# Sparse first FFN on eight group buffers, with late weights and zeros sent later and its block stages one tick further apart

## The reference, cut to what matters

```python
x = L0_attn_x
x = x + 0.5 * ffn(layernorm(x))
x = x + attn(layernorm(x))
x = x + 0.5 * ffn(layernorm(x))

def ffn(x):   # 8 experts, 2 of them per token
    w = softmax(x @ router_w + router_b)                    # [.., 8]
    gate = top-2 of w, divided by their sum, 0 elsewhere
    h = gelu(einsum('btd,nde->btne', x, W1) + b1)           # 256 -> 128 per expert
    out = einsum('btne,nef->btnf', h, W2) + b2              # 128 -> 256
    return sum(out * gate[..., None], axis=-2)
```

## Time and profile before

| what | before |
|---|---|
| median of 3 runs | 2168.53 us |
| the profiled execution | 2167.86 us |
| its span, first to last instruction | 2166.1 us |
| sparse first layer (ends with the last output product) | 0 to 424 us |
| first scatters, then batch 0's end of scatters | 30 us, 84 us |
| batch 1's, batch 2's end of scatters | 190 us, 313 us |
| mean granted PE clock over the span | 0.957 |

### The profile page before, as it was taken

One profiled execution on the slowest core, in us unless ns is written; L12 is line 12 of the kernel. 1 busy time (PEld: TensorE's weight loads), 2 busy tenths in 40 slices (PEclk: granted clock), 3 DMA queues, 4 the chain that ended last, 5 costly groups with the idle time before them and its releaser, 6 DMA issues.

```text
span 2166.1 us, 39513 instructions
## 1 busy us (share of the span) xinstructions
PE 1909.9 (88%) x12240; PEld 1479.5 (68%) x12240; DVE 1526.4 (70%) x5026; ACT 1220.3 (56%) x3005; POOL 1195.1 (55%) x1376
## 2 busy tenths in 40 slices
PE   3576777888998988988988988988999999999998
PEld 3576766856666656656656656655767688888887
DVE  4566577676685685685686686686674478888887
ACT  3354566847546547547547547547556545555554
POOL 5785666467276276277277277277245444444444
PEclk9987888989998999999999999999999999999999
DMA  9755567411030031031031031031013101111110
GB/s 329 279 195 187 208 218 225 170 52 38 6 101 27 1 103 30 1 103 30 1 103 31 1 103 30 1 103 30 1 45 127 34 23 40 40 40 40 40 40 30
DMA packets 106696, 173.74 MB, mean 80 GB/s; under 512 B 13409, under 2 KB 65017, under 8 KB 105593
## 3 DMA queue, kind: packets, MB, share of 16 engines
q1 hardware_dynamic: 83304, 117.37, 16.0%
q0 software_dynamic: 20736, 52.52, 7.9%
q10 hardware_dynamic: 2448, 1.33, 0.2%
HBM read 80.33 MB, written 90.84 MB: 79 GB/s over the span
## 4 chain that ended last, share of the span: by engine, by line
PE 43%; POOL 20%; DVE 16%; issue 14%; ACT 3%; DMA 2%; SPq 1%; DVEq 0%; POOLq 0%; ACTq 0%
PE bank L705 7%; PE bank L707 6%; PE bank L706 6%; PE bank L977 4%; PE bank L959 4%; PE bank L948 4%; POOL prob L1933 3%; PE bank L988 3%; POOL spots_d L1882 3%; POOL hs_d L1920 3%; PE bank L919 3%; DVE x L1516 2%; POOL y_row L1904 2%; POOL z_row L1904 2%; DVE st L1353 1%
## 5 line engine op out<-in xcount | busy, mean ns | idle before, releaser
L1933 POOL TENSOR_TENSOR prob<-prob,rden 128x512 f32<-128x512 f32 x320 | 337.5, 1057 | 483.3 <-DVE rden L1722 480.2
L1264 ACT ACTIVATE prob<-prob,nmax 128x256 f32<-128x256 f32 x512 | 256.3, 504 | 365.4 <-DVE nmax L1704 365.2
L1704 DVE CUSTOM_DVE_ANT_0 prob<-bank,mask 128x256 f32<-128x256 f32 x512 | 195.1, 418 | 154.5 <-PE bank L948 154.2
L1591 DVE SCALAR_TENSOR_TENSOR xb<-bank,gate,xb 128x256 f32<-128x256 f32 x512 | 211.9, 476 | 55.6 <-PE bank L707 54.9
L959 PE MATMUL bank<-ident,prob 128*128 128x128 f32 x1280 | 201.9, 282 | 49.0 <-POOL prob L1933 49.0
L959 PEld LDWEIGHTS bank<-ident,prob 128*128 128x128 f32 x1280 | 157.3, 144 | 110.2 <-POOL prob L1933 69.6
L948 PE MATMUL bank<-kT,qT 64*128 64x256 f32 x1024 | 211.6, 434 | 23.2 <-DVE nmax L1704 18.4
L1858 POOL TENSOR_TENSOR hl<-hf,hh 128x512 fp32r<-128x512 f32 x128 | 164.6, 1291 | 113.5 <-ACT hh L1088 108.8
L1716 DVE COPY probT<-bank 128x512 f32<-128x512 f32 x160 | 110.2, 689 | 119.9 <-PE bank L959 119.8
L1087 ACT ACTIVATE hf<-bank,b1s 128x512 f32<-128x512 f32 x128 | 88.2, 689 | 171.2 <-PE bank L707 167.7
L977 PE MATMUL bank<-probT,V 128*64 128x128 f32 x2048 | 172.6, 290 | 0.5 <-ACT oT_s L1280 0.5
(11 more groups left out here) (254 smaller groups left out, 5511.7 us busy)
## 6 DMA issues: line engine op xcount, KB each, us to landing
xin<-spots_d SPq DMA_DIRECT2D x85, 256.0 KB, 3.9
made_d<-yout SPq DMA_DIRECT2D x85, 256.0 KB, 3.2
xb<-in_L_attn_x SPq DMA_DIRECT2D x16, 512.0 KB, 4.4
x<-in_L_attn_x SPq DMA_DIRECT2D x8, 1024.0 KB, 6.3
x_d<-x SPq DMA_DIRECT2D x8, 1024.0 KB, 5.0
xb<-x_d SPq DMA_DIRECT2D x16, 512.0 KB, 3.8
out<-xb SPq DMA_DIRECT2D x16, 512.0 KB, 2.9
spots_d<-zeros SPq DMA_DIRECT2D x24, 256.0 KB, 3.0
```

The lines of the kernel that those rows point to most:

```text
L1264: act.activation(prob[j % NP][:, h, :], src, ACT.Exp, bias=nmax[:, j % 4, h:h + 1], scale=-1.0 if light else 1.0, accum_out=den[:, j % 4, ...
L1591: dve.scalar_tensor_tensor(out=x, in0=bank[ob][:, (t % 2) * D:(t % 2 + 1) * D], scalar=gate[:, k % 2, t, e:e + 1], in1=x, op0=ALU.mult, op ...
L1704: ins = dve.tensor_tensor_reduce(prob[j % NP][:, h, :], bank[g % NS][:, 0:KEYS], mask[:, which, :], -1.0, 3e38, ALU.add, ALU.min, nmax[:, ...
L1933: pool.tensor_tensor(prob[j % NP][:, :, :], prob[j % NP][:, :, :], rden[:, j % 4, :].unsqueeze(2).broadcast_to([P, 2, KEYS]), ALU.mult).th ...
```

## The change

- The groups get eight buffers `xb` in place of four. A group from the ninth on is loaded six ticks ahead of its own tick, once the scatters of the group eight before have landed; groups 6 and 7 share space with staged weights and wait for their split.
- The groups' ticks move: 3 apart up to group 6, then 4, 6 and 5 apart. The last group's tick is 61 in place of 63, `STEP0` 24 in place of 25.
- A group's stages are further apart: `rstd` 1, norm 2, transposes 3, logits 4, route 5, exponential 6, spots on PE 6, spots and gates on DVE 7, scatters 8 to 11.
- A step's stages: transposes and `xh` 0, the copy of W1 and `xl` 1, hidden 2, gelu 3, `hl` 4, output 5, `yout` 6, store 7; `xh` and `xl` get a third buffer. There are 117 ticks in place of 115. On PE the order in a tick is transposes, output, hidden, group jobs.
- SP: the staged attention weights go to tick 7, the broadcast of b2 from ACT's queue to SP's tick 11, the three transfers of zeros to ticks 13, 36 and 60, the late attention weights to ticks 82 and 86, the store of the split weights from tick 12 to 90, the load of row 0 from 24 to 70.
- Three of row 0's projections are made in ticks 112 to 114, in place of two. The copy of token numbers into `yr` comes after the ticks.

The diff, cut to its core (buffer indices `% 4` become `% 8` for `xb`, and `% 2` become `% 3` for `xh` and `xl`, in all other places too):

```diff
-        xb = [at(f"xb{i}", [P, TG, D], F32, xt_off + i * TG * D * 4) for i in range(4)]
+        xb_off = [xt_off + i * TG * D * 4 for i in range(4)] + [y_off, y_off + TG * D * 4] + [yr_off + (T * (D + 1) + i * TG * D) * 4 for i in range(2)]
+        xb = [at(f"xb{i}", [P, TG, D], F32, off) for i, off in enumerate(xb_off)]
...
-        xh = [at(f"xh{i}", [P, C, BLK], F32R, x1_off + (T * D + i * C * BLK) * 4) for i in range(2)]
-        xl = [at(f"xl{i}", [P, C, BLK], F32R, x1_off + (T * D + (2 + i) * C * BLK) * 4) for i in range(2)]
+        x_off = [x1_off + T * D * 4, x1_off + (T * D + 2 * C * BLK) * 4, yr_off]
+        xh = [at(f"xh{i}", [P, C, BLK], F32R, x_off[i]) for i in range(3)]
+        xl = [at(f"xl{i}", [P, C, BLK], F32R, x_off[i] + C * BLK * 4) for i in range(3)]
...
-        STEP0 = 25
-        TICKS = STEP0 + STEPS + 5
-        GROUP_AT = (0, 4, 8, 12, 16, 20, 24, 27, 30, 34, 38, 43, 48, 53, 58, 63)
+        STEP0 = 24
+        TICKS = STEP0 + STEPS + 8
+        GROUP_AT = (0, 3, 6, 9, 12, 15, 18, 22, 26, 30, 36, 41, 46, 51, 56, 61)
         def group_at(tau, after):
...
         DOT0 = at_ticks(11, 12, 13, 14, 15, 16, 17, 18)
-        QKV0 = {STEP0 + STEPS + 1 + i: i for i in range(2)}
+        QKV0 = {STEP0 + STEPS + 3 + i: i for i in range(3)}
         def tick_jobs(tau):
-            jobs = [("aT", k, pr) for k in group_at(tau, 2) for pr in range(2)]
+            jobs = [("aT", k, pr) for k in group_at(tau, 3) for pr in range(2)]
             jobs += [("alg", k, 0) for k in group_at(tau, 4)]
             jobs += [("apos", k, 0) for k in group_at(tau, 6)]
             jobs += [("zt", 0, i) for i in ZT0.get(tau, ())]
...
         def attn_jobs(u):
-            jobs = [("qkv", b, i) for b, i in due(u, qkv_slot, 25) if (b, i) not in ((0, 0), (0, 1))]
+            jobs = [("qkv", b, i) for b, i in due(u, qkv_slot, 25) if (b, i) not in ((0, 0), (0, 1), (0, 2))]
             jobs += [("srow", b, i) for b, i in due(u, srow_slot, 4)]
...
         def sent(engine, n):
-            for k in range(2 * BATCH[n][1] - 4, 2 * BATCH[n][1]):
-                engine.wait_ge(s_sc[k % 4], 128 * (k // 4 + 1))
+            for k in range(2 * BATCH[n][0], 2 * BATCH[n][1]):
+                engine.wait_ge(s_sc[k % 8], 128 * (k // 8 + 1))
...
-                if k >= 4:
-                    sp.wait_ge(s_sc[k % 4], 128 * (k // 4))
-                sp.dma_start(xb[k % 4][:, :, :], half(x_v, k)).then_inc(s_xa[k % 4], 16)
+                if k in (6, 7):
+
+                    sp.wait_ge(s_wlo, 4)
+                if k >= 8:
+                    sp.wait_ge(s_sc[k % 8], 128 * (k // 8))
+                sp.dma_start(xb[k % 8][:, :, :], half(x_v, k)).then_inc(s_xa[k % 8], 16)
             def pads(n):
...
             group_load(3)
-            sp.dma_start(wqkv_st[:, :, :], wqkv.rearrange("(c p) n -> p c n", p=P)).then_inc(s_wld[4], 16)
-            sp.wait_ge(s_const, CONST)
-            for n in range(len(BATCH)):
-                sp.dma_start(spots_d[n][SPARE[n]:SPARE[n] + (E - 1) * BLK, :].rearrange("(j p s) d -> p j (s d)", p=P, s=BT),
-                             zeros[:, :, :].rearrange("p s d -> p (s d)").unsqueeze(1).broadcast_to([P, E - 1, BT * D])).then_inc(s_spare, 16)
-            sp.dma_start(wqh_s[:, :, :], wq_h.rearrange("(c p) n -> p c n", p=P)).then_inc(s_late, 16)
-            sp.dma_start(wkvh_s[:, :, :], wkv_h.rearrange("(c p) n -> p c n", p=P)).then_inc(s_late, 16)
-            sp.dma_start(wol_s[:, :, :], wo_l.rearrange("(c p) n -> p c n", p=P)).then_inc(s_late, 16)
-            sp.dma_start(woh_s[:, :, :], wo_h.rearrange("(c p) n -> p c n", p=P)).then_inc(s_late, 16)
             for tau in range(TICKS):
-                for s_ in step_at(tau - 5):
+                for s_ in step_at(tau - 7):
                     block_store(s_)
                 for s_ in step_at(tau + 3):
                     block_load(s_)
-                for k in group_at(tau, 10):
-                    if k + 4 < GROUPS:
-                        group_load(k + 4)
-                if tau == 12:
+                for k in group_at(tau + 6, 0):
+                    if k >= 4:
+                        group_load(k)
+                if tau == 7:
+                    sp.dma_start(wqkv_st[:, :, :], wqkv.rearrange("(c p) n -> p c n", p=P)).then_inc(s_wld[4], 16)
+                if tau == 11:
+                    sp.dma_start(b2_all[:, :, :].rearrange("p e n -> p (e n)"), b2.rearrange("(a e) n -> a (e n)", a=1).broadcast_to([P, E * D])).then_inc(s_b2all, 16)
+                if tau in (13, 36, 60):
+
+                    if tau == 13:
+                        sp.wait_ge(s_const, CONST)
+                    n = (13, 36, 60).index(tau)
+                    sp.dma_start(spots_d[n][SPARE[n]:SPARE[n] + (E - 1) * BLK, :].rearrange("(j p s) d -> p j (s d)", p=P, s=BT),
+                                 zeros[:, :, :].rearrange("p s d -> p (s d)").unsqueeze(1).broadcast_to([P, E - 1, BT * D])).then_inc(s_spare, 16)
+                if tau == 82:
+                    sp.dma_start(wqh_s[:, :, :], wq_h.rearrange("(c p) n -> p c n", p=P)).then_inc(s_late, 16)
+                    sp.dma_start(wkvh_s[:, :, :], wkv_h.rearrange("(c p) n -> p c n", p=P)).then_inc(s_late, 16)
+                if tau == 86:
+                    sp.dma_start(wol_s[:, :, :], wo_l.rearrange("(c p) n -> p c n", p=P)).then_inc(s_late, 16)
+                    sp.dma_start(woh_s[:, :, :], wo_h.rearrange("(c p) n -> p c n", p=P)).then_inc(s_late, 16)
+                if tau == 90:
                     sp.wait_ge(s_wlo, 6)
                     sp.dma_start(w1_d, w1_s[:, :, :, :, :].rearrange("p e w c f -> p (e w c f)").bitcast(F32)).then_inc(s_wst, 16)
                     for n in range(2):
                         sp.dma_start(w2_d[n], w2_s[n][:, :, :].rearrange("p e n -> p (e n)").bitcast(F32)).then_inc(s_wst, 16)
                     sp.dma_start(b2_d, b2_s[:, :].bitcast(F32)).then_inc(s_wst, 16)
-                if tau == 24:
+                if tau == 70:
                     attn_load(0, x_v)
             sp.wait_ge(s_bh, STEPS)
             attn_load(1, x_v)
...
                     block_turn(s_)
-                for what in todo[0:1]:
+                for s_ in step_at(tau - 5):
+                    block_out(s_)
+                for s_ in step_at(tau - 2):
+                    block_hidden(s_)
+                for what in todo:
                     job(*what)
-                for s_ in step_at(tau - 1):
-                    block_hidden(s_)
-                for what in todo[1:]:
-                    job(*what)
-                for s_ in step_at(tau - 3):
-                    block_out(s_)
             for u in slots():
                 todo = attn_jobs(u)
                 if is_item(u):
...
                 act.wait_ge(s_bT, s_ + 1)
-                if s_ >= 2:
-                    act.wait_ge(s_bh, s_ - 1)
-                act.activation(xh[s_ % 2][:, :, :], view(s_ % 2, "p (c n) -> p c n", c=C), ACT.Copy).then_inc(s_bhi)
+                if s_ == 2:
+
+                    act.wait_ge(s_wlo, 2)
+                if s_ >= 3:
+                    act.wait_ge(s_bh, s_ - 2)
+                act.activation(xh[s_ % 3][:, :, :], view(s_ % 2, "p (c n) -> p c n", c=C), ACT.Copy).then_inc(s_bhi)
             def block_gelu(s_):
                 act.wait_ge(s_bh, s_ + 1)
...
             for tau in range(TICKS):
+                for s_ in step_at(tau - 1):
+                    w1_copy(s_)
+                for s_ in step_at(tau - 3):
+                    block_gelu(s_)
                 for s_ in step_at(tau):
-                    w1_copy(s_)
                     block_hi(s_)
-                for s_ in step_at(tau - 1):
-                    block_gelu(s_)
-                for k in group_at(tau, 1):
+                for k in group_at(tau, 2):
                     group_norm(k)
                 for what in tick_jobs(tau):
                     evac(*what)
...
-                    group_route(x)
-                    return
-                if kind == "apos":
-                    group_spots(x)
-                    return
                 pv = bank[jbank(job)]
...
             for tau in range(TICKS):
-                for s_ in step_at(tau - 4):
+                for s_ in step_at(tau - 1):
+                    block_lo(s_)
+                for s_ in step_at(tau - 6):
                     block_left(s_)
-                for s_ in step_at(tau):
-                    block_lo(s_)
                 for k in group_at(tau, 0):
                     group_stats(k)
-                for what in tick_jobs(tau):
-                    evac(*what)
-                for k in group_at(tau, 5):
-                    group_gates(k)
-                for k in group_at(tau, 6):
+                for k in group_at(tau, 7):
+                    group_spots(k)
                     if last_of_batch(k):
                         batch_table(batch_of_group(k))
-                for k in group_at(tau, 8):
```

(30 more changed lines are left out.)

17 lines of the change are left out of this document (7 added, 10 removed).

## The result

The changed kernel takes 2133.8 us in the median of 4 runs (2127.63 to 2134.26), the kernel before took 2168.0 on the same chip: a ratio of 0.9836, 95% interval 0.9817 to 0.9855. The forecast was 2144, with a range of 2122 to 2166. The profiled execution took 2133.56 us, so the sum of the prediction is judged against 2133.6 - 2167.9 = -34.3 us.

A forecast was written before the change was run, and what follows sets the result against it. Between 84 and 313 us the prediction took POOL's work plus what POOL waits for as the bound. Its terms summed to -24.0 us, taking 2167.9 to 2143.9 us (2144), with a range of 2122 to 2166.

The forecast's parts named there:

- Batch 0, +2.5: Up to 84 us: with groups three ticks apart, two scatters of group 4 delay the first batch's completion by 2.5 us.
- POOL's work, -5.1: From 84 us to the last scatter: two scatters, two `hl` and one `rstd` fewer on POOL, saving 5.1 us.
- POOL's waits, -22.4: From 84 us to the last scatter: POOL's 43.4 us of waits shrink to 21, bounds 0 and -35.
- Third batch, +1: After the last scatter: pads and block load stand as before, with one tick less PE work in hand; +1, bounds 0 and 3.
- gathers into the hole, -2.5: At the third batch: two of POOL's gathers fill its wait for `hl`, saving 2.5 us, bounds 0 and -5.
- Row 0's stretch and last steps, -5: From 333 to 424 us: `xl` and `hl` get one more tick, cutting PE's 12.3 us of waits; -5, bounds 0 and -12.
- late transfers, +6: Store and late weights ahead of block loads on SP's queue: 5 us and 1 us exposed, zeros nothing; bounds 0 and 26.
- The lighter queue buys nothing: From the first scatter to 84 us: POOL has no idle time to win, so less DMA load gains nothing.
- B: Between batches POOL stays fed, 8 us of waits left in place of 21, late transfers hidden: 2125 us; chance 0.20.
- C: Between batches PE becomes the bound through half-clock ticks, 36 us of waits left in place of 21: 2159 us; chance 0.15.
- D: Ticks 82 to 95: late transfers on SP's queue take 35 us, all exposed in place of 6: 2173 us; chance 0.08.
- E: POOL's waits for the exponential return as waits for `hl`, so 43 us stay: 2166 us; chance 0.12.

The follow-up runs named there:

- The square: Four combinations, all with eight buffers: group and block stages each of before or changed. Both before 2144.4, only group changed 2166.7 (2155.4), only block changed 2168.1, both changed 2133.8 us.
- the middle transfers: Changed kernel with the store of split weights and late attention weights in tick 17, zeros of batches 2 and 3 in ticks 18 and 19: 2126.1 us, 0.9810.

## Why the prediction was right, point by point

- **What bounds.** Right: the stretch was POOL's work and what POOL waited for, and it shrank by that. Shown by eight buffers alone (22 us, all between the batches). The run with four buffers inside the change loses 16 us, but 11 of them before the batches' stretch; from batch 0's end on POOL waits only 11.4 us for others, though SP stands before the group loads again. So with the change's stages in place the buffers count mostly at the start, which the prediction did not see.
- **Batch 0, +2.5.** Its last scatter, the 34th of all, ended at 84.64 in place of 84.1, **+0.5**: the two scatters of group 4 cost their 2.5, and some was given back by the first scatter, at 28.97 in place of 30.07 (I had taken 0 there, bounds -3.7 and +2.5). With the old tick plan the batch was complete at 80.3, so closer groups cost 4.3 us here, not 2.5.
- **POOL's work, -5.1.** What is left of -42.2 after batch 0 and the waits is -42.2 - 0.5 + 37.2 = **-5.5**. Right, and for its reason: from 84 to 271 POOL makes 95 scatters, 46 `hl` and 9 `rstd`, where it made 97, 48 and 10 from 84 to 313.
- **POOL's waits, -22.4.** Measured 43.4 - 6.2 = **-37.2**, past the bound of -35. This is the term that was mis-sized, by 14.8 us. I kept 9 us for the exponential, and 1.1 were left; I kept 8 for `rstd`, and none was. These shares were guesses on how many waits would outlive one more tick of distance, and next to none did.
- **Its reason.** Half right. I put the gain on eight buffers and on the distance of the group stages, each by itself. The square shows that the distance of the group stages by itself loses 22 us. The order within a tick matters as much: with the group stages close, PE's jobs first got 21.6 of 34.3 us back without any stage being moved.
- **Third batch, +1, and gathers into the hole, -2.5.** From last scatter to block 54 it took 17.2 us in place of 15.1, **+2.1**. The two gathers did go into the hole (286.57 and 287.87, ahead of the `hl` for which the first gather of before waited); what they gave would show behind block 54 and can't be told there. The pads' lump still stands in the stretch: spread, it takes 284.36 - 268.54 = 15.8.
- **Row 0's stretch and last steps, -5, more ticks, +1.5, late transfers, +6.** Sum +2.5; measured from block 54 to the last output product 99.5 in place of 95.2, **+4.3**, and 1.5 more behind it. PE's waits of before in the stretch that answers to 271 to 388, 313 to 424 us:

```profile
PE bank L705 <- POOL hl L1886: 8.3, 7, 2.2
PE bank L705 <- DVE xl L1491: 7.6, 10, 1.4
PE bank L830 <- DMA xin<-spots_d: 7.1, 1, 7.1
```

  For `hl` and `xl` PE waits 8.6 + 3.6 after, 3.7 less than the 15.9 here; for `xin` 12.2, 5.1 more. So these waits shrank about as far as predicted, all of it in `xl`. The time did not follow: with the block stages of before, the stretch from block 54 to the last output product takes 98.7 us in place of 99.5, so the tick more bought nothing there, where -5 + 1.5 had been forecast. The late transfers, taken out, give 5.5 us in this stretch and 7.7 by the medians (2133.8 to 2126.1), or 3 to 5 by the run that has them all early; 6 was a fair size. The stop behind the store was not 5 us but 2.18. (The fit that the prediction takes from the Trainium skill, DMA: Bandwidth & Descriptors, section Anatomy of one DMA, is stated there for DMAs that GpSimd issues; the store is SP's, and no run shows when it landed.)
- **"The lighter queue buys nothing", "moving the store frees nothing."** The first was wrong in one thing, the order: with the new tick plan the early transfers cost 10 us at block 0, because they stand ahead of group 4's load. How full the queue is did not matter, and so the second was right: the middle transfers with a DMA share of 0.98 from 30 to 84 us turned block 0 at 89.5 as well.
- **The rivals.** B (2125) had the right size of waits, 8 us, and was wrong in that the late transfers would be hidden; 2144 - 13 = 2131 by its first half alone. PE's clock was 0.90, 0.80 and 0.91 where it had been 0.84, 0.74 and 0.82. The Trainium skill, TensorE: Matmul & The Clock Gate, section HAM oscillation, says that a PE kept fed keeps its clock; but the other runs do not tie the rise to the waits for `xin`. From 84 to 270 us the clock was 0.82 before and 0.89 after. Eight buffers alone left 11.8 us of these waits and had 0.84; the change with the block stages of before left 4.9 us and had 0.85; with four buffers it kept 30.1 us (15.9 of them before block 0) and had 0.90. The runs with the block stages and PE's order of before all lie at 0.82 to 0.85, those with the change's at 0.87 or more; which of the two does it, and how, was not tested. What the clock gave cannot be parted from the rest, since POOL sets the pace. C (PE as bound) did not happen. D happened in its place at about a fifth of its size (6 to 8 of 35 us). E did not happen here, but it is what happens with the block stages of before: 30.9 us of waits for `hl` and 2155.4 us.
- **The listed signs.** Right: group-load waits gone, exponential under 10 us (1.1), `xin` under 8 us at the second batch (4.5 at block 23). Too cautious: last scatter 288 (270.7), last output product near 400 (387.4).

The sum as it came: 0.5 - 5.5 - 37.2 + 2.1 + 4.3 + 1.5 = -34.3 us. Against the -24.0 of the prediction, POOL's waits made 14.8 more and batch 0 and POOL's work 2.4 more; the part behind the last scatter, +7.9 in place of +1, gave 6.9 back. That makes the 10.3 us between 2143.9 and 2133.6. The total is thus nearer than its parts, by luck.

## What to carry to other kernels

When one in-order queue holds both loads that may have to wait for a buffer and loads that are needed now, give the first kind more buffers before anything else: here that alone made 22 us. Before stages are moved apart by ticks, look at the order within a tick: the products that feed a chain of other engines in the same tick go first, and a chain moved by one tick can collide with another chain, so move one and read the waits' new names. Cut a lump of DMA issues into twos and issue them behind the load that is needed in that tick (3 to 5 us here); moving the lump as it is only moves the hole. Ask of every load what stands ahead of it in its queue's order, before asking how full the queue is.

## What the runs showed of the hardware

- Issue time on SP's queue is a cost of its own. Eight pads took 7.55 us to issue at one place and 7.63 at another, so from one start to the next it is about 1 us. Two at a time (1.18 and 1.28 us) are not much cheaper: less the second one's own 0.35 us it is 0.83 and 0.93 from start to start. A block load, whose row is also a computed number, is 0.34 us long by itself.
- How full the queue is did not matter in itself. From 30 to 84 us the DMA share was 0.48 in the changed kernel and 0.98 with the transfers in the middle (windows of the two), and block 0 was turned at 89.5 in both. With the transfers ahead of the ticks it was turned at 99.5 in the new tick plan and at 89.3 in the kernel before, whose groups are four ticks apart. In the new plan the 10 us come from the order in SP's queue: the middle transfers stand behind group 4's load, and its statistics begin at 39.3 us with them, 39.4 in the changed kernel and 56.7 with the transfers ahead.
